# Retention and mixture-of-experts layer: the sums of states between the k and the q projection, and VectorE's state update ahead of its copy of q

## The reference

```python
q = (x @ W_q.T).reshape(b, t, h, dh)
k = (x @ W_k.T).reshape(b, t, h, dh)
v = (x @ W_v.T).reshape(b, t, h, dh)
...
attn = jnp.einsum('bihd,bjhd->bhij', q, k) * decay[None] / scale
y = jnp.einsum('bhij,bjhd->bihd', attn, v)
mean = y.mean(axis=(1, 3), keepdims=True)
var = y.var(axis=(1, 3), keepdims=True)
yn = (y - mean) / jnp.sqrt(var + EPS)
yn = yn.reshape(b, t, dm) * gn_weight + gn_bias
return yn @ W_o.T
...
x = x + _L0_attn_ref(_layernorm(x, axis=-1), ...)
x = x + _L0_ffn_ref(_layernorm(x, axis=-1), ...)
```

## Time and profile before

| | before |
|---|---|
| median of 3 runs | 428.78 us (428.75, 428.78, 429.99) |
| the profiled execution | 431.59 us, of which its span is 429.8 us |
| PE busy | 419.1 us, 98% of the span, 6232 matmuls |
| PEld busy | 380.5 us |
| DVE busy | 335.3 us, 78% |
| ACT busy | 219.2 us, 51% |
| POOL busy | 87.9 us, 20% |
| share of the chain that ended last | PE 96%, issue 1%, DVE 1%, DMA 1% |

### The profile page before, as it was taken

One profiled execution on the slowest core, in us unless ns is written; L12 is line 12 of the kernel. 1 busy time (PEld: TensorE's weight loads), 2 busy tenths in 40 slices (PEclk: granted clock), 3 DMA queues, 4 the chain that ended last, 5 costly groups with the idle time before them and its releaser, 6 DMA issues.

```text
span 429.8 us, 14531 instructions
## 1 busy us (share of the span) xinstructions
PE 419.1 (98%) x6232; PEld 380.5 (89%) x6232; DVE 335.3 (78%) x791; ACT 219.2 (51%) x420; POOL 87.9 (20%) x78
## 2 busy tenths in 40 slices
PE   7998999999999989999999999999999999999997
PEld 5987899999998989998989988899888998888996
DVE  7888689876987788987798887978879878856423
ACT  3566667555754568345257325483344834346530
POOL 3062634532344232650510000100001000000000
PEclk9999999999999999999999999999999999999999
DMA  8554444434351232315450015100142001120011
GB/s 262 192 150 139 126 151 116 114 104 133 123 169 51 87 115 89 101 53 195 158 187 2 2 49 190 56 0 1 49 152 91 0 1 49 49 98 0 2 50 49
DMA packets 19769, 39.79 MB, mean 93 GB/s; under 512 B 3040, under 2 KB 5376, under 8 KB 19200
## 3 DMA queue, kind: packets, MB, share of 16 engines
q1 hardware_dynamic: 19280, 38.31, 27.5%
q10 hardware_dynamic: 432, 0.66, 0.5%
HBM read 30.55 MB, written 8.41 MB: 91 GB/s over the span
## 4 chain that ended last, share of the span: by engine, by line
PE 96%; issue 1%; DVE 1%; DMA 1%; POOL 0%; ACT 0%; DVEq 0%
PE bank L434 54%; PE bank L443 13%; PE bank L526 7%; PE bank L444 7%; PE bank L556 4%; PE bank L571 4%; PE bank L540 3%; PE bank L505 2%; PE bank L589 1%; DMA xin<-xa 1%; PE bank L647 0%; PE bank L461 0%; PE bank L452 0%; DVE xlo L1311 0%; DVE ln_st L1298 0%
## 5 line engine op out<-in xcount | busy, mean ns | idle before, releaser
L434 PE MATMUL bank<-x2lo,sw_hi 128*128 128x512 f32 x128 | 50.5, 394 | 0.0
L434 PE MATMUL bank<-x2hi,sw_lo 128*128 128x512 f32 x128 | 50.2, 392 | 0.0
L434 PE MATMUL bank<-x2hi,sw_hi 128*128 128x512 f32 x128 | 50.1, 392 | 0.0
L443 PE MATMUL bank<-w_both,ehi 128*128 128x512 f32 x124 | 45.1, 397 | 0.0
L887 ACT ACTIVATE sil<-bank,s1b 128x512 f32<-128x512 f32 x32 | 22.0, 687 | 45.0 <-PE bank L434 44.9
L443 PE MATMUL bank<-sw_both,ghi 128*128 128x512 f32 x124 | 44.9, 396 | 0.0
L1199 DVE STREAM_TRANSPOSE x2t<-xl 32x256 f32<-32x256 f32 x96 | 41.8, 436 | 1.8
L768 ACT ACTIVATE kexp<-bank 64x256 f32<-64x256 f32 x64 | 24.2, 378 | 30.9 <-PE bank L505 30.2
L1029 DVE TENSOR_TENSOR pm<-bank,msk 128x512 f32<-128x512 f32 x64 | 39.5, 679 | 0.0
L434 PE MATMUL bank<-xhi,wqkv_hi 128*128 128x256 f32 x128 | 38.0, 297 | 0.1
L906 ACT ACTIVATE ehi<-xres 128x512 fp32r<-128x512 f32 x32 | 20.3, 633 | 33.1 <-PE bank L444 32.6
(11 more groups left out here) (154 smaller groups left out, 1152.0 us busy)
## 6 DMA issues: line engine op xcount, KB each, us to landing
w_raw<-w SPq DMA_DIRECT2D x16, 256.0 KB, 3.3
xres<-xs SPq DMA_DIRECT2D x16, 256.0 KB, 3.4
x_scratch<-xres SPq DMA_DIRECT2D x16, 256.0 KB, 3.3
xl<-x_scratch SPq DMA_DIRECT2D x8, 512.0 KB, 4.5
xr<-x_scratch SPq DMA_DIRECT2D x4, 1024.0 KB, 4.8
xin<-xa SPq DMA_DIRECT2D x15, 256.0 KB, 3.0
out<-xr SPq DMA_DIRECT2D x7, 512.0 KB, 2.6
xin_t<-xt SPq DMA_DIRECT2D x13, 256.0 KB, 2.6
```

What stands on the lines that cost most here:

```text
L434: mm = nc.tensor.matmul(o, w[c][l], x[c][r], start=first and c == 0 and j == 0, stop=last and c == n - 1 and j == 2)
L443: nc.tensor.matmul(o.rearrange("p (k d) -> p k d", k=2), hi, w[c], start=c == 0, stop=c == n - 1, skip_group_check=True)
```

## The change

Two lines move. On PE, `state_sums(h)` goes from behind the q projection to a place between the k and the q projection, ahead of `head_means` where that stands there. On DVE, `add_state(h)` goes ahead of `decay_q(h + 1)`. Nothing is added or removed.

```diff
                 project_k(h + 1)
+                state_sums(h)
                 if b and s == 0:
                     pe.wait_ge(pm_ready, h * PAIRS + 1)
                     head_means(b - 1, p_bank[0])
                 project_q(h + 1)
-                state_sums(h)
                 from_scores(h, True)
...
                     mask_scores(h, range(PAIRS))
                     decay_k(h + 1)
+                    add_state(h)
                     decay_q(h + 1)
-                    add_state(h)
                     if b and s == 0:
                         gn_spread(b - 1, p_bank[0])
```

## The result

| | before | after |
|---|---|---|
| median, 7 runs each | 429.78 us | 431.96 us |
| lowest to highest | 428.75 to 430.61 | 431.31 to 432.92 |
| ratio, 95% interval | | 1.0053 (1.0037 to 1.007) |
| the profiled execution, its span | 431.59, 429.8 us | 431.68, 429.9 us |

The account below looks back on a forecast made before the run. PE was taken as the bound, its time set by matmul switches and issue gaps: 428.78 + 4.6 for switches - 2.0 given back by gaps = 431.4 us, range 428.2 to 433.8.

Parts of the forecast that it names:

- the switches: On PE, one run on array pieces becomes two per pass: 4.6 us slower over 15 passes, bounds 2.4 to 4.8.
- PE is the bound and no other engine's time counts: PE is busy 98% and never waits for another engine from 16 to 196 us, so earlier DVE states shorten nothing.
- what is queued behind the copy of q: On DVE, work behind q's copy moves by about 0.3 us; taken to cost nothing, as PE never waits for it.
- The head means' step: Head means behind the sums in h = 4, 8, 12: 0.07 us more each, bounded by nothing and 0.15.
- The bullet on L571: Scores times v, now behind the full-array q projection: 1.03 instead of 0.90 us, +0.13 a pass.
- the one on the sums: The sums (L540) follow a full-array projection in either order: 0.84 us, no change.
- The gaps: PE's issue gaps, read as late loads of 254-instruction blocks: slow q matmuls between small groups give back 2.0, between 1.1 and 2.6.
- the kind for which I took 0.4 off: Blocks made faster, running from late L526 over k and the sums in 4.0 us: new stalls up to 0.9 us.
- Fast enough loads to give everything back: Rival: most blocks load in time, switches cost 2.4 to 3.5, 2.5 to 3.5 come back: 428.0 to 430.0 us; chance 0.22.
- a switch below 0.1 us: Rival: weight loads run ahead of the switch, a pass pays under 0.1 us: 427.3 us or less; chance 0.07.
- The earlier sums: Forecast: v copies leave 0.9 us in hand in h = 2. Rival: sums wait for ACT, 4.5 us more; shared chance 0.09.
- The clock: Granted clock 1.00 in all four windows (2.4 GHz), so the clock was taken to play no part.

Follow-up runs that it names:

- the swap: Kernel before with its two groups of small matmuls swapped, scores times v ahead of the sums, both behind q: 437.21 against 430.25 us, ratio 1.0188.
- the halves: Against the kernel before, sums of chunks 0 and 1 between k and q, those of chunks 2 and 3 behind q: 433.56 against 430.94 us, ratio 1.0061.
- the shift: Kernel before with two of four warm-up matmuls replaced by 16 of 2 columns, shifting PE's instruction stream: 435.76 against 430.94 us, ratio 1.0111.
- the twelve other passes: Kernel before with the change made in the 12 passes other than h = 2, 10 and 12: 433.93 us, ratio 1.0065.

## Why the prediction was right, and where it was off

**The sign and the size.** Forecast 431.4 us, 2.6 above the median then known; measured 2.2 us above its median of 7, inside the range. Two errors partly cancel in that: the switches cost 0.1 more than I had, and about 0.5 more came back. The 2.0 I took for the second was a choice between bounds of 1.1 and 2.6, so it is in part luck that the time came out within 0.6 us.

**PE is the bound and no other engine's time counts.** Right for both whole kernels. But I argued from it that the state additions, sooner, shorten nothing, and that was incomplete: with PE's order changed, DVE's half keeps 1.4 us at L583 away. I had put what is queued behind the copy of q at 0.3 us later, and taken it as free because no row showed PE waiting for it. In h = 4, 8 and 12 that queue holds what L583 waits for, and I had not looked at how much room it has there, nor at either half of the change by itself.

**The switches.** Forecast 12 x 0.33 + 3 x 0.20 = 4.6, measured 12 x 0.31 + 3 x 0.33 = 4.7. q behind the sums took 1.62 (forecast 1.63) and L571 1.03 (1.03), L540 stayed at 0.83. The head means' step was off: they pay 0.19 behind the sums, above my bound of 0.15. The bullet on L571 prices it behind full-array work and the one on the sums leaves them at 0.84; the swap and the halves show what joins the two, that the first group of a run pays the 0.13.

**The gaps.** The mechanism held: they stand at multiples of 254 counted instructions in every trace, they moved with the stream, each ends 1.2 to 1.6 us behind a packet of instructions, and those of h = 10 and h = 12 went in the first trace after the change. In the second trace of the same kernel 0.56 us is left in h = 12, so that gap is shorter with the change and not always gone. For the profiled execution I gave too little back: I forecast 433.6 for it and 431.68 came. I had counted the idle time that the waits view names, 4.8 us, where the groups around it are lengthened by 6.3. For usual executions I had taken 2.0 given back; by the subtraction above it was about 2.5. The new gap of 0.68 us in h = 14 is of the kind for which I took 0.4 off. How long a load takes varies from one execution to the next: the gap of h = 12 is gone after the change in one trace, 0.56 us in the other, and 1.13 us where the change was made in three passes.

**The rivals.** Fast enough loads to give everything back did not come, nor a switch below 0.1 us. The earlier sums did not wait for ACT: the 0.9 us in hand held. One group of matmuls further ahead they did, as the sums ahead of k show. By the rows, entering and leaving once more costs 0.31 to 0.33 us. That agrees with the drain on a change of mode of which the Trainium skill speaks (TensorEngine Tiling, Key Properties). The 175 ns of the Trainium skill, TensorE: Matmul & The Clock Gate, Single matmul latency, made it an estimated 0.35; that figure is given there for one matmul by itself, not for a change of mode.

**The clock.** I left it out, as the windows of the earlier trace rows are all at 1.00. Both profiled executions bear that out, but not all others: see the last section.

**Open.** That a gap is a late load of instructions rests on the blocks' size, on the shift and on the times of the packets; no run changed the load itself. Why a packet begins 0.7 us behind the begin of a block in one place and 2.4 in another is not shown, and with it the length of a gap can't be forecast.

## What to carry to other kernels

Count the runs of like matmuls on TensorE, not only the matmuls: here each further run on pieces of the array between full-array work cost 0.31 to 0.33 us, and an order that splits one run in two must earn that back on a wait that the profile shows. Where issue gaps stand a multiple of one number of instructions apart, look at how long PE takes for a block: here a block with many small matmuls was done before the next had come, and an edit that mixes in slow ones bought some of its price back. And move the halves of an edit apart on the chip: two moves on two engines, each slower or useless alone, can hold each other's cover.

## What the hardware showed beyond what was expected

A block of 254 counted instructions is one packet of 16 KB on the queue named instruction, and PE went on 1.2 to 1.6 us after that packet's end wherever it had run out. The idle time so made is named "issue" in every view, in the middle of groups of like matmuls.

A gap can cost nearly as much again behind it. In three traces the granted clock fell to 1.2 GHz for 3.4 us: behind a gap of 1.87 us (half of the sums at each place), behind one of 1.69 us (the twelve other passes, where the v projection of h = 12 took 2.75 instead of 1.54 us), and behind two gaps of 0.66 and 0.67 us with a wait of 0.23 us between them (the swap). But the gap of 2.33 us in the kernel before and one of 1.69 us with DVE's half alone left the clock at 1.00, so the length of a gap does not decide it by itself, and what does is not shown.

The same shows in times. Of the 73 executions of the kernel before beside the experiments, the 585 us one left out, 18 have a mean granted clock of 0.995 or 0.996, and on each of the three chips (of four) where they occur their median lies 1.8 to 2.7 us above that of the others. An estimate from the traces agrees: 3.4 us at half the clock lose 1.7 us. None of the 12 of the whole change beside them has it, which may be a part of what it gives back; at the rate of the kernel before three would have been expected, and 12 are too few to say.

In the shifted kernel the 32 trace records of matmuls with 2 columns, ahead of all work, took 0.21 us each, against 0.06 for the head means; no run shows why.
